# Image attention: the last 128 token keys and the context keys turned by a DMA transpose

## The reference

```python
x = layer_norm(image_embeds, ln1_g, ln1_b)      # context
l = layer_norm(latents, ln2_g, ln2_b)           # tokens
q = l @ Wq
kv_in = jnp.concatenate([x, l], axis=1)
kv = kv_in @ Wkv
k, v = jnp.split(kv, 2, axis=-1)                # then 16 heads of 64
w = jnp.einsum('bhqd,bhkd->bhqk', q * scale, k * scale)
w = jax.nn.softmax(w.astype(jnp.float32), axis=-1).astype(q.dtype)
out = jnp.einsum('bhqk,bhkd->bhqd', w, v)
return out.transpose(0, 2, 1, 3).reshape(B, S_lat, INNER) @ Wo
```

## Time and profile before

| what | value |
|---|---|
| median of three runs | 1663.16 us |
| lowest, highest | 1662.12, 1663.86 us |
| the profiled execution, its own time | 1667.16 us |
| its span | 1665.3 us |
| TensorE busy | 1445.0 us, 87% of the span |
| DVE, POOL, ACT busy | 1110.9, 877.9, 780.5 us |
| instructions | 36883 |
| first hardware queue (SyncE's transfers) | 33831 packets, 59.83 MB, 12.2% of 16 engines |

### The profile page before, as it was taken

One profiled execution on the slowest core, in us unless ns is written; L12 is line 12 of the kernel. 1 busy time (PEld: TensorE's weight loads), 2 busy tenths in 40 slices (PEclk: granted clock), 3 DMA queues, 4 the chain that ended last, 5 costly groups with the idle time before them and its releaser, 6 DMA issues.

```text
span 1665.3 us, 36883 instructions
## 1 busy us (share of the span) xinstructions
PE 1445.0 (87%) x13680; PEld 985.4 (59%) x13849; DVE 1110.9 (67%) x2918; ACT 780.5 (47%) x1566; POOL 877.9 (53%) x1308
## 2 busy tenths in 40 slices
PE   5999999999999897977888889979977777789987
PEld 3777777777777775755566555534544344434545
DVE  5889788878777773544764667854446567487753
ACT  4777667767766661632233355554234434211111
POOL 5789889978776693363335653422033332153330
PEclk8999999999999999998899899999987979789998
DMA  7333232111221111250000000000000000000000
GB/s 279 103 90 86 86 97 50 49 44 45 61 49 44 52 51 57 58 182 1 1 1 1 9 9 1 2 1 1 1 1 1 0 1 1 1 1 1 7 7 14
DMA packets 35479, 64.31 MB, mean 39 GB/s; under 512 B 7535, under 2 KB 25042, under 8 KB 34147
## 3 DMA queue, kind: packets, MB, share of 16 engines
q1 hardware_dynamic: 33831, 59.83, 12.2%
q0 software_dynamic: 1472, 2.12, 0.4%
HBM read 30.64 MB, written 12.66 MB: 26 GB/s over the span
## 4 chain that ended last, share of the span: by engine, by line
PE 35%; DVE 10%; ACT 4%; POOL 3%; issue 2%; DVEq 0%; ACTq 0%; POOLq 0%
PE banks L520 9%; PE banks L2210 3%; PE banks L2196 2%; PE banks L3058 2%; PE banks L3001 1%; PE banks L2723 1%; PE banks L2717 1%; PE banks L2163 1%; PE banks L495 1%; DVE work L2293 1%; PE banks L2199 1%; PE banks L1763 1%; PE banks L305 1%; PE banks L2985 1%; PE banks L1687 1%
## 5 line engine op out<-in xcount | busy, mean ns | idle before, releaser
L1059 POOL TENSOR_TENSOR work<-work 128x512 bf16<-128x512 f32 (+1 forms) x512 | 358.7, 723 | 76.4 <-ACT work L952 75.5
L835 DVE TENSOR_REDUCE work<-banks 128x1 f32<-128x666 f32 x256 | 216.4, 846 | 64.9 <-PE banks L752 62.2
L959 ACT ACTIVATE work<-banks,work 128x666 f32<-128x666 f32 x256 | 208.1, 813 | 30.3 <-DVE work L835 23.3
L952 ACT ACTIVATE work<-banks 128x512 f32<-128x512 f32 x256 | 152.8, 597 | 146.0 <-PE banks L763 145.7
L460 POOL TENSOR_TENSOR norm_room<-norm_room,minus_half 128x4 f32<-128x4 f32 (+1 forms) x56 | 53.1, 949 | 294.7 <-DVE norm_room L435 170.0
L763 PE MATMUL banks<-const,work 128*128 128x128 f32 x1024 | 159.2, 278 | 15.5 <-ACT work L952 12.3
L752 PE MATMUL banks<-work 128*128 128x154 bf16 (+1 forms) x898 | 160.4, 295 | 9.7 <-DVE work L909 1.6
L520 PE MATMUL banks<-work,weights_b 128*128 128x512 bf16 (+1 forms) x830 | 150.1, 337 | 13.6 <-ACT work L1348 7.0
L752 PEld LDWEIGHTS banks<-work 128*128 128x128 bf16 x1024 | 96.0, 98 | 80.6 <-DMA work<-work 2.8
L2293 DVE TENSOR_REDUCE work<-banks 128x2 f32<-128x308 f32 x192 | 87.0, 472 | 82.0 <-PE banks L2163 56.2
L791 PE MATMUL banks<-work 128*128 128x65 bf16 (+1 forms) x3840 | 136.6, 192 | 3.0 <-POOL work L1059 1.8
(11 more groups left out here) (463 smaller groups left out, 3294.7 us busy)
## 6 DMA issues: line engine op xcount, KB each, us to landing
work<-work SPq DMA_DIRECT2D x128, 166.5 KB, 2.8
sorted<-in_pads SPq DMA_DIRECT2D x10, 838.5 KB
weights_b<-in_weights SPq DMA_DIRECT2D x1, 4120.0 KB, 13.4
work<-scratch SPq DMA_DIRECT2D x64, 64.0 KB, 1.9
weights_b<-in_weights SPq DMA_DIRECT2D x1, 2824.0 KB, 12.3
weights_a<-in_weights SPq DMA_DIRECT2D x1, 2056.0 KB
weights_a<-in_weights SPq DMA_DIRECT2D x1, 2050.0 KB, 9.9
work<-work SPq DMA_DIRECT2D x32, 64.0 KB, 1.9
```

Of the source, the lines that this page charges most:

```text
L835: ve.tensor_reduce(self.neg_max[i % 4], self.slot[i % 2][:, 0:KEYS0], AX_X, ALU.max, negate=True).then_inc(self.mark("max"))
L952: ac.activation(self.probs_t[u % 2][:, h, 0:4, j * P:(j + 1) * P], self.bank_a.rearrange("p (t n) -> p t n", t=4), ACT.Copy).then_inc(self ...
L959: ac.activation(self.probs[i % 3], self.slot[i % 2][:, 0:KEYS0], ACT.Exp, bias=self.neg_max[i % 4]).then_inc(self.mark("exp"))
L1059: po.tensor_tensor(parts[:, :, :, 0], exact, parts[:, :, :, 1], ALU.subtract).then_inc(self.mark(event, i - 3))
```

## The change

ACT writes the exponentials of a round into one of four buffers, which are padded from 666 to 704 words. TensorE turns only the first three blocks of 128 token keys (`DIRECT` = 3). The other 282 keys, 128 of tokens and 154 of the context, are not turned by TensorE. POOL splits them into their two bf16 halves where they lie, before they are turned (`low_c`), and SyncE issues one `dma_start_transpose` on them: 128 rows of 640 bf16 values (320 words), from SBUF to SBUF. In the result a tile holds 64 keys (`HALF_KEYS`), and each key takes two partitions: one with the low part of its weight and one with the high part. There are five such word tiles (`WORDS0`).

The values for these keys must stand twice, on both partitions of each key. They are kept as rows in a new buffer `v_rows` and copied by six transfers of SyncE for each group, to every second partition. For a word tile two products are enough, one with the high and one with the low part of the values, since both parts of the weights are in the same tile.

The turned blocks go to eight buffers (`TURNS`). The exponential of round i waits until the turned blocks of round i-4 have landed, since it writes over their source. SyncE's list is written in the loop's order now: the copies of a group are spread over steps 1, 5 and 7, and between them stands a transposing transfer for each round. The shared block of the last context keys and all that served it are gone: POOL's gathering, the transposes L775, DVE's two operations and the three products of 264 columns. DVE's eviction of the fifth block is gone too.

The core of the diff:

```diff
+HALF_KEYS = P // 2
+DIRECT = QT - 1
+WORDS0 = -(-(KEYS0 - DIRECT * P) // HALF_KEYS)
+TURNS = 8
...
+    def image_turn_pe(self, pe, sub):
+        pe.wait_ge(*self.at("exp", sub + 1))
+        ps = self.bank(pe, 4, "kept_a", sub)
+        for t in range(DIRECT):
+            m = pe.transpose(ps[:, t * P:(t + 1) * P], self.probs[sub % 4][:, t * P:(t + 1) * P], self.eye)
+        m.then_inc(self.mark("turned_a"))
...
         for j in (0, 1):
-            for t in range(KT0 - 1):
-                for which, (of_values, of_probs, width) in enumerate(orders):
+            sub, out = 4 * u + 2 * h + j, self.out_heads[:, 2 * j + h, :]
+            for t in range(DIRECT):
+                for which, (of_values, of_probs, width) in enumerate(((0, 1, D0 + 1), (0, 0, D0 + 1), (1, 1, D0))):
...
+            pe.wait_ge(*self.turned_in(sub))
+            for t in range(WORDS0):
+                for of_values, width in ((0, D0 + 1), (1, D0)):
+                    m = pe.matmul(out[:, 0:width], self.words_t[sub % TURNS][:, t, :], v[:, DIRECT + t, of_values, h, 0:width],
+                                  start=False, stop=(h, j, t, of_values) == (1, 1, WORDS0 - 1, 1), skip_group_check=True)
...
             if i < SUBS:
-                if i >= 3:
-                    ac.wait_ge(*self.at("turned_b", i - 1))
-                    ac.wait_ge(*self.at("gathered", i - 3))
+                if i >= 4:
+                    ac.wait_ge(*self.at("turned_a", i - 3))
+                    ac.wait_ge(*self.turned_in(i - 4))
                 ac.wait_ge(*self.at("max", i + 1))
-                ac.activation(self.probs[i % 3], self.slot[i % 2][:, 0:KEYS0], ACT.Exp, bias=self.neg_max[i % 4]).then_inc(self.mark("exp"))
+                ac.activation(self.probs[i % 4][:, 0:KEYS0], self.slot[i % 2][:, 0:KEYS0], ACT.Exp, bias=self.neg_max[i % 4]).then_inc(self.mark("exp"))
...
             if 1 <= i < SUBS + 1:
+                whole = self.probs[(i - 1) % 4][:, DIRECT * P:KEYS0]
                 po.wait_ge(*self.at("exp", i))
-                po.tensor_copy(self.rest[u % 2][:, 32 * (2 * j + h):32 * (2 * j + h + 1)], self.probs[(i - 1) % 3][:, KEYS0 - 32:]).then_inc(self.mark("gathered", i - 1))
+                po.tensor_tensor(self.halves(whole)[:, :, 0], whole, self.halves(whole)[:, :, 1], ALU.subtract).then_inc(self.mark("low_c", i - 1))
...
+        for i in self.image_steps():
+            n = (i - 1) // 8 + 1
+            if i % 8 in (1, 5, 7) and n < GROUPS0:
+                self.image_heads_sp(sp, n, (1, 5, 7).index(i % 8))
...
+            if 1 <= i < SUBS + 1:
+                sub = i - 1
+                if sub >= TURNS:
+                    sp.wait_ge(*self.at("weighed", (sub - TURNS) // 2 + 1))
+                sp.wait_ge(*self.at("low_c", sub))
+                words = self.probs[sub % 4][:, DIRECT * P:].bitcast(BF16)
+                sp.dma_start_transpose(self.words_t[sub % TURNS], words).then_inc(self.mark(f"dma_turn{sub % TURNS}", n=16), 16)
...
+            sp.wait_ge(*self.at("v_low", 3 * n + 3))
+            if n >= 3:
+                sp.wait_ge(*self.at("weighed", 2 * (2 * n - 4)))
...
+            for word in (0, 1):
+                for h, own in ((0, top), (1, bottom)):
+                    sp.dma_start(v[word::2, DIRECT + h:DIRECT + WORDS0 - 1:2, :], rows[own, 0:2, :]).then_inc(self.mark("dma_values", n=16), 16)
+                sp.dma_start(v[word:2 * CTX_REST:2, DIRECT + WORDS0 - 1, :], rows[0:CTX_REST, 2, :]).then_inc(self.mark("dma_values", n=16), 16)
```

More of the change, by code:

```diff
@@ L895, in value_pieces @@
     def value_pieces(self):
-        return [(KT0 - 2, slice(0, CTX - 32), slice(2 * P, 3 * P))] + [(KT0 - 1 + j, slice(64 * j, 64 * j + 64), slice(3 * P, 4 * P)) for j in (0, 1)]
-    def rest_due(self, i):
-        t = i - 2
-        return t // 4 - 1 if t % 4 == 1 and 1 <= t // 4 <= UNITS else None
+        return [(slice(0, P), 1, slice(2 * P, 3 * P)), (slice(0, CTX_REST), 2, slice(3 * P, 4 * P))]
     def image_lows_ve(self, ve, n, part):
@@ L919, in image_lows_ve @@
             k, c0, width = self.k_parts, (0, SEQ)[part - 1], (SEQ, CTX)[part - 1]
[L920 removed]
+            ve.wait_ge(*(self.at("k_high", 2 * n + 1) if part == 1 else self.at("v_kept", 3 * n + 2)))
             ve.tensor_tensor(k[:, 1, c0:c0 + width], side[:, 0:width], k[:, 0, c0:c0 + width], ALU.subtract).then_inc(self.mark("k_low"))
         if part == 2:
[L923 removed]
+            for rows, tile, src in self.value_pieces():
+                v = self.v_rows
                 ve.tensor_tensor(v[rows, tile, 1, :, 0:D0], side[rows, src].rearrange("p (h d) -> p h d", h=2), v[rows, tile, 0, :, 0:D0], ALU.subtract).then_inc(self.mark("v_low"))
```

196 lines of the change are left out of this document (77 added, 119 removed).

## The result

The changed kernel takes 1780.03 us (1771.67 to 1786.17, 4 runs) beside 1663.43 for the kernel before (1662.12 to 1663.86): ratio 1.0699, 95% interval 1.0655 to 1.0744. It is slower, as forecast, but by 117 us where I gave 38. The profiled execution took 1779.24 us, its span 1777.4. Ratios are always against runs of the kernel before on the same chip, whose median was between 1655 and 1663 us.

What follows compares the result with a forecast made beforehand. TensorE bound the kernel before; SyncE's queue would bound the changed one. Its 0.90 us a group over the period (+29 us) and the padding (+9) give +38 us on 1663.2: 1701 us, range 1635 to 1790.

Steps and rivals of the forecast that it cites:

- TensorE, -1.66 us a group: Image attention: fewer transposes and context products, 32 more value products; TensorE saves 1.66 us a group, 53 us over 32.
- POOL 0.83 and 0.66 us: POOL's two subtractions in a round, of 384 and 282 columns: 1.49 us together, 0.17 less than before.
- DVE, ACT and POOL are worth nothing: Work saved on these three engines gains no time by itself, since none was the bound; it keeps them below TensorE.
- That SyncE's queue becomes the bound: Image attention: SyncE's added issues fill its queue and hide TensorE's 53 us; chance 0.53, at 1701 us.
- TensorE's share falling: Sign in the new profile: TensorE's busy share of the image attention stage falls from 94% to near 87%.
- The queue's group, 8.89 + 8 T = 18.89 us: SyncE's issues and pauses for eight rounds, T being one transposing issue: 0.90 us over the period, +29 us over 32 groups.
- T = 1.25: Issue time in us of one transposing transfer on SyncE, set a step above the 1.07 of a load of x.
- padding: Ten padding issues on SyncE, 0.88 + 0.04 us each, formerly in the queue's idle time: +9 us.
- The present group, 17.99 us: Eight rounds of image attention in the kernel before, from 573.55 / 255 = 2.249 us a round.
- (a): TensorE stays the bound because a transposing transfer issues like any copy: 1610 to 1650 us, chance 0.24.
- (d): A draw: SyncE's queue and TensorE both full, the 53 us spent on waits between them: 1663 us, chance 0.08.
- (b): Transposing transfers land too late for the exponential four rounds on, deciding from 3.0 us: 1733 us at 4.0, chance 0.10.
- (c): The DMA engines fill up with small pieces, 1.32 of 2.249 us a round expected: 1758 us if full, chance 0.05.

Runs made afterwards that it cites:

- half kernel: Changed kernel with transposing transfers on even rounds only and doubled values copied for the first three groups only: 1664.00 us, ratio 1.0042.

## Why the forecast was right in direction and wrong in size

**TensorE, -1.66 us a group: right.** 1.65 measured where nothing else bounds. The starts of the half kernel's matmuls hold the unit prices, 0.030 us for a product (19 in 0.57) and 0.12 for a transpose (three in 0.36):

```profile
405.57 0.43 PE L805 MATMUL banks<-work 128*128 128x65 bf16 x9
405.85 0.46 PE L810 MATMUL banks<-work 128*128 128x65 bf16 x10
406.14 0.52 PE L772 MATMUL banks<-const,work 128*128 128x128 f32 x3
406.50 0.73 PE L764 MATMUL banks<-work 128*128 128x512 bf16 x4
```

**POOL 0.83 and 0.66 us: right** (0.834 and 0.662). DVE, ACT and POOL are worth nothing: right.

**That SyncE's queue becomes the bound: right for the kernel, but my own numbers did not carry it** (see the present group below). Issues end to end, the exponentials waiting for DMA, TensorE's share falling: all as named, though to 79% where I said 87%.

**The queue's group, 8.89 + 8 T = 18.89 us: this step failed.** Summed over groups 5 to 28 it is 22.4 us, +3.5:

| term | forecast | measured |
|---|---|---|
| eight transposing issues | 10.0 | 10.7 (median 1.227, mean 1.33) |
| six copies of values | 3.6 | 4.45 |
| queries and keys with the swap's wait | 4.73 | 5.5 |
| pauses | 0.56 | 1.5 |
| padding | counted apart, 9 us in all | 0.25 |

T = 1.25 was a good median, and no use as a mean: some issues take up to 2.59 us. The values' copies were priced by the keys' median, 0.597; the rows of L1115 and L1116 say 0.622 and 0.851, and the mean of L1115 in these groups is 0.69. The pause behind an issue was read between instructions that don't wait (0.04 us); ahead of an instruction that waits for two semaphores, the first of them by a wait instruction of its own, it is 0.10, as from 418.46 to 418.56, and nine a group are of this kind; the rest of the 1.5 are pauses of 0.05 and the 0.3 of waits for producers. The swap's landing wait grew from 0.86 to 1.12. The largest single piece is none of the prices that I argued about: in groups 5 to 28, 36 of 511 issues of any line take 0.33 to 1.54 us longer than the median of their line, 1.25 us a group together (in the kernel before it was 1 of 174). It isn't the amount of data, since with a fifth of it they cost 1.41 us a group; what causes them is open. The rest are small prices, nearly all of them a little low. The sum came out 16% short, and since the loss is the difference of the queue and the present period, a small share of the queue is a large share of the loss.

**The present group, 17.99 us: misread.** With the right 18.8 (the whole stage) to 19.1 (groups 5 to 28) the queue's 18.89 and the padding's 9 us would have forecast +2 to +12 us, next to no change. So the two errors pulled in opposite ways, and that the forecast had the direction right is luck. Rightly done, (22.38 - 19.10) x 32 = +105.

**What I left out: the first group, +12 us.** I named the wait for the queries' swap but not what lay in front of it. The 4.1 MB of weights cost the kernel before at most 1 us (first group 16.1 us, sliced 15.2), because what waited for the swap was not on its path. After the change the exponential is behind that wait. The +105 above counts 3.3 us for this group too, so the first group adds 9 to it.

**The rivals.** (a) falls: 1.23 us is twice a copy. (d), a draw, falls. (b), landing, is not the bound, though landing at 3.5 us lies above the 3.0 from which I said it would decide: five buffers moved the wait to the keys. (c), full DMA engines, is rejected as the bound by the fifth of the data, but its load was priced low: 0.78 us a round for the transposing transfers and the values, where the shares say 0.65 x 2.79 - 0.24 x 2.35 = 1.25. The mean is 0.65, and a stretch of a few us can read over one (1.12 from 408.20 to 411.00, in the last rows below). What delayed rounds was rather a big transfer beside them.

On the size of a transposing transfer the Trainium skill's page "DMA: Bandwidth & Descriptors" (the table behind "Why a DMA increments its semaphore by 16 and not by 1") led to an estimate of 1.07 to 1.59 us with 32 cycles a tile; the median, 1.227, lies between, but from 8 to 48 tiles it moves by 0.06 us only, so the growth by tiles is not there in the issue. The rule of "Advanced Engine Details and Errata" (X-Bar Transpose), as fast as regular DMAs, is near the landing (3.5 us against the keys' 3.2), and for the issue the trace doesn't agree with it: 1.227 us is twice a copy's.

## What to carry to other kernels

Sum a queue with mean prices by shape, with the pause of a waiting instruction, and compare it with a period counted from a first and a last event whose number you have checked. A transfer that becomes part of each round puts on the path whatever delays it: look for every large transfer in the stage, on any queue, even those that cost nothing today. To relieve a queue, cut instructions, not bytes: a fifth of the transposed bytes took the ratio from 1.0699 to 1.0562, six issues fewer in a group to 1.0185.

## What the hardware showed that I had not expected

- The issue of a transposing transfer from SBUF to SBUF is nearly free of its size: median 1.182 us for 128 columns, 1.206 for 384, 1.227 for 640, 1.240 for 768. The landing does depend: 2.3 us for 128 columns, 2.8 for 384, 2.7 to 3.5 for 640 (medians).
- In groups 5 to 28 of the changed kernel 36 of 511 issues took 0.33 to 1.54 us more than their line's median, and 43 of 511 with a fifth of the data; in the kernel before it was 1 of 174.
- Two products on 52 partitions among products on 128 cost 0.19 us more than on 128: TensorE's next start comes 0.12 us later in place of 0.03, once on the way in and once on the way out.
- A copy of 26 x 264 values takes longer to issue (0.851 us) than one of 64 x 2 x 264 (0.622).
- A transfer behind one padding of 330 KB kept ACT waiting 4.28 us; moving such transfers to another engine's queue did not help.
- TensorE's granted clock stood at 1.00 in the stage of the kernel before (29 to 629 us), but for one stretch of 3.4 us. In the changed kernel it fell to the lower of its two levels, 1.2 in place of 2.4 GHz, in 18 stretches between 57 and 735 us, 61 us in all. One of them goes from 406.6 to 410.0 us, where TensorE is busy throughout; ahead of it lies a wait of 1.52 us for the exponential:

```profile
405.39 0.74 PE L759 MATMUL banks<-work 128*128 128x512 bf16 x4 [1.52 <-ACT work L947]
```

```profile
404.40:408.20 3.80, 2.59 (x18) 2.13 (x19) 1.88 (x3) 2.88 (x5) 2.58 (x4) 0.79 0.43 96
408.20:411.00 2.80, 2.80 (x47) 2.25 (x46) 0.85 (x1) 1.25 (x4) 2.22 (x4) 0.68 1.12 111
411.00:420.00 9.00, 7.52 (x112) 5.61 (x111) 5.41 (x12) 5.28 (x11) 6.78 (x10) 1.00 0.71 155
```

  At half the clock the 61 us hold at most 31 us less of TensorE's work, an estimate from these levels. How much of that stands in the loss beside a full queue was not measured; the 0.3 us a group that SyncE waits for producers speaks for little.
